# Two fused convolution layers on one core: another order for the first and the last image, the x1 chunks of both in places of their own, and one preparation step of every image a round earlier

## The reference, cut to what matters

```
# layer 0: x1 = x + conv0(group_norm(x)), with v = group_norm(x)
f     = relu(Wc @ v + bc)                         # 512 -> 128 channels (1x1)
gk1   = relu(mean(v) @ Wc.T + bc); g_kern = gk1 * Wkk + bkk
sk    = relu(Wc @ max_over_16x16_cells(v) + bc)   # 3x3 cells
dynW  = relu(Wck @ stack([g_kern, sk]) + bck)     # a 3x3 kernel of each image's own
y     = conv3x3(f, dynW) + b_ad                   # 128 -> 128
x1    = x + (Wf @ y + bf)                         # 128 -> 512 (1x1)
# layer 1: 32 groups of 16 channels, weights of each group's own
out   = x1 + conv3x3(group_norm(x1), kernels, groups=32)
```

## Time and profile before

| | us |
|---|---|
| median of three runs | 3616.0 (3615.7 to 3616.5) |
| the profiled execution | 3616.31 |
| its span, first to last instruction | 3614.6 |
| PE busy | 3498.8 (97%) |
| DVE busy | 2532.3 (70%) |
| ACT busy | 2109.9 (58%) |
| POOL busy | 965.3 (27%) |
| DMA, share of 16 engines | 68.5% |

### The profile page before, as it was taken

The page is one execution under the profiler, slowest core; times in us unless marked ns, Lnnn a source line. Parts: engine busy times, 40 slices in busy tenths (PEclk is TensorE's granted clock), DMA queues, the critical chain, the costliest instruction groups (busy, mean ns, idle before and its releaser), DMA issues.

```text
span 3614.6 us, 60228 instructions
## 1 busy us (share of the span) xinstructions
PE 3498.8 (97%) x18688; PEld 2789.1 (77%) x18688; DVE 2532.3 (70%) x5365; ACT 2109.9 (58%) x3559; POOL 965.3 (27%) x1039
## 2 busy tenths in 40 slices
PE   5799999999999999999999999999999999999996
PEld 4677877777877778877778777778777778777785
DVE  7676777776767677777667777767777777776742
ACT  4365555665555665655655556655556655556654
POOL 2033222232222232222332222322222322223323
PEclk9899999999999999999999999999999999999998
DMA  5467767677767667767677667677676777676666
GB/s 122 142 193 190 190 178 185 200 195 192 185 180 195 191 184 193 190 183 197 189 188 190 186 178 207 197 190 186 178 191 194 188 195 186 182 199 187 170 156 158
DMA packets 317577, 666.88 MB, mean 184 GB/s; under 512 B 58863, under 2 KB 288242, under 8 KB 288645
## 3 DMA queue, kind: packets, MB, share of 16 engines
q1 hardware_dynamic: 317317, 663.34, 68.5%
HBM read 355.00 MB, written 308.28 MB: 184 GB/s over the span
## 4 chain that ended last, share of the span: by engine, by line
PE 90%; issue 5%; DVE 4%; DMA 1%; POOL 0%; DVEq 0%; ACT 0%; SPq 0%; POOLq 0%; ACTq 0%
PE pb L853 15%; PE pb L855 15%; PE pb L854 15%; PE pac L853 7%; PE pd L853 7%; PE pd L855 7%; PE pd L854 7%; PE pac L854 6%; PE pac L855 6%; PE pac L925 2%; PE pac L862 1%; DVE x1b L764 1%; PE ps L918 1%; DMA big<-x 0%; DVE va L596 0%
## 5 line engine op out<-in xcount | busy, mean ns | idle before, releaser
L407 POOL TENSOR_TENSOR hl<-un,hl 128x384 f16<-128x384 f32 x1024 | 937.6, 916 | 2570.2 <-ACT hl L432 2566.6
L432 ACT ACTIVATE hl<-un 128x384 f16<-128x384 f32 x1024 | 539.0, 526 | 427.8 <-PE pb L855 361.7
L428 ACT ACTIVATE un<-big,b_t,s_t 128x384 f32<-128x384 f32 x1024 | 709.7, 693 | 16.1 <-DMA big<-x_rows 16.1
L853 PE MATMUL pb<-fh,dynh 128*128 128x480 f32 (+1 forms) x1440 | 548.2, 381 | 0.0
L855 PE MATMUL pb<-fh,dynl 128*128 128x480 f32 (+1 forms) x1440 | 545.3, 379 | 0.0
L854 PE MATMUL pb<-fl,dynh 128*128 128x480 f32 (+1 forms) x1440 | 544.4, 378 | 0.0
L774 DVE SCALAR_TENSOR_TENSOR big<-pd,kout,big 96x768 f32<-96x768 f32 x256 | 258.8, 1011 | 382.6 <-PE pd L855 382.6
L853 PE MATMUL pd<-hl,k_h 128*96 128x384 f16 x1536 | 507.0, 330 | 18.8 <-POOL hl L407 18.8
L774 DVE SCALAR_TENSOR_TENSOR big<-pb,kout,big 96x768 f32<-96x768 f32 x256 | 258.9, 1011 | 351.8 <-PE pb L855 351.8
L853 PE MATMUL pb<-hl,k_h 128*96 128x384 f16 x1536 | 504.9, 329 | 0.0
L854 PE MATMUL pd<-hl,k_h 128*96 128x384 f16 x1536 | 504.8, 329 | 0.0
(11 more groups left out here) (115 smaller groups left out, 5241.6 us busy)
## 6 DMA issues: line engine op xcount, KB each, us to landing
big<-x SPq DMA_DIRECT2D x128, 1152.0 KB, 9.8
x_rows<-x1b SPq DMA_DIRECT2D x128, 1152.0 KB, 5.6
big<-x_rows SPq DMA_DIRECT2D x128, 1152.0 KB, 12.7
out<-big SPq DMA_DIRECT2D x128, 1152.0 KB, 6.2
big<-x_rows SPq DMA_DIRECT2D x256, 192.0 KB, 13.2
x_rows<-mrow SPq DMA_DIRECT2D x64, 96.0 KB, 1.9
big<-kt SPq DMA_DIRECT2D x4, 288.0 KB, 9.7
big<-kt SPq DMA_DIRECT2D x2, 192.0 KB, 11.0
```

What stands on the lines that cost most here:

```text
L407: pool.tensor_tensor(hl[:, g % HL_RING, 1, :, 1:W + 1], un[:, g % U_RING], hl[:, g % HL_RING, 0, :, 1:W + 1], ALU.subtract).then_inc(hl_lo, 1)
L428: act.activation(un[:, g % U_RING], t_slot(g // GQ)[:, g % GQ], ACT.Identity, bias=b_t[:, g:g + 1], scale=s_t[:, g:g + 1]).then_inc(u_done, 1)
L432: act.activation(hl[:, g % HL_RING, 0, :, 1:W + 1], un[:, g % U_RING], ACT.Copy).then_inc(hl_hi, 1)
L853: pe.matmul(acc, high_w, high_x, start=start, stop=False)
```

## The change

It has three parts.

- **Step 0.** Its four chunks stand behind rounds 0 to 3 (`C_AT_FIRST`), ahead of the preparation of image 1. x1 of chunks 1 to 3 goes to the three tile buffers, so `residual` no longer waits for the DMA there; it waits for the split weights of layer 1 (`k_lo`), whose staging lies in those buffers, and still for `square`. The last maxima of image 0 and `centred` move behind the first `x_low`. `kernel_inputs` and the image's own kernel move on PE behind tiles 1 and 3 of stage A, with psum of their own (three banks of `pbd`, which joins `pb` and `pd`); `dyn_high`, `dyn_low` and the scale of layer 1's weights come behind stage A.
- **Step 31.** Its chunks stand behind rounds 0, 2, 4 and 6 (`C_AT_LAST`), with x1 in the free x places. Means, statistics, `write_means` and the tiles' loads of image 31 are issued in the rounds; two of its tiles go to x places. The last chunk is stored in four pieces.
- **Every step.** `centred` is a function of its own; a copy of 128x36 becomes one of 128x1. `prep_scaled` 0 and 1 go from round 10 to round 9, and `prep_scaled` 2 from round 11 to round 10.

The diff, cut:

```diff
@@ -48,6 +48,8 @@
...
 C_AT = {0: 0, 4: 1, 8: 2, 11: 3}
+C_AT_FIRST = {0: 0, 1: 1, 2: 2, 3: 3}
+C_AT_LAST = {0: 0, 2: 1, 4: 2, 6: 3}
...
+SQUARE_AFTER_LAST = {5: 0, 9: 1, 13: 2, 17: 3}
+SUMS_LAST = 7
+MEANS_LAST = 8
+GROUP_STATS_LAST = 10
+SPREAD_LAST = 12
...
-PREP_SCALED_AT = 10
+PREP_SCALED_AT = 9
...
@@ -225,7 +232,10 @@
...
-        dyn_acc = pac[:, :, 0:3 * CM]
+        def dyn_acc(n):
+
+            return pbd[:, 1:4, 0:3 * CM] if isinstance(n, int) and n == 0 else pac[:, :, 0:3 * CM]
...
+        def t_slot(n, c):
+
+            if is_step(n, N - 1):
+                if c < 2:
+                    at = 4 * PX + c * GQ * BW
+                    return x_flat[:, at:at + GQ * BW].rearrange("p (j b w) -> p j b w", j=GQ, w=W)
+                return tb[:, c - 1, :, :, :]
             return tb[:, T_SLOT[c], :, :, :]
+
+        def x1_home(n, c):
+
+            if is_step(n, 0) and c:
+                return tb[:, c - 1].rearrange("p j b w -> p (j b w)")[:, 0:OR_ * BW].rearrange("p (k m) -> p k m", k=OR_)
+            if is_step(n, N - 1) and c:
+                return xb[:, x_slot(c, 0), :].rearrange("p (k m) -> p k m", k=OR_)
+            return x1b[:, 0]
...
+        def chunks_of(d, more):
+            return C_AT_FIRST if not d else C_AT if more else C_AT_LAST
...
-                if T_SLOT[c] in T_SLOT[:c]:
+                if is_step(n, 0) and c < Q - 1:
+                    sp.wait_ge(x1_out[c + 1], 16)
+                    sp.wait_ge(sq_done, Q)
+                if is_step(n, N - 1):
+                    if c >= 2:
+                        sp.wait_ge(stored[c - 1], written)
+                elif T_SLOT[c] in T_SLOT[:c]:
                     sp.wait_ge(stored[T_SLOT.index(T_SLOT[c])], written)
                 else:
                     sp.wait_ge(stored[Q - 1 if c == 0 else c], written)
@@ -323,7 +361,13 @@
...
+            def store_pair(n, p):
+                at = 2 * p % GQ
+                sp.wait_ge(out_done, n * PAIRS + p + 1)
+                sp.dma_start(out[n, p // PER_CHUNK, :, at * BW:(at + 2) * BW],
+                             t_slot(n, p // PER_CHUNK)[0:M6, at:at + 2].rearrange("p j b w -> p (j b w)")).then_inc(stored[p // PER_CHUNK], 16)
...
-                if d:
+                    if d:
+                        store(n - 1, 0)
+                    write_x1(n, 1)
+                    if d:
+                        load_t(n - 1, Q - 1)
+                        store(n - 1, 1)
+                    write_x1(n, 2)
+                    if d:
+                        store(n - 1, 2)
+                    write_x1(n, 3)
+                else:
+                    write_x1(n, 1)
                     store(n - 1, 0)
-                write_x1(n, 1)
-                if d:
+                    write_x1(n, 2)
                     load_t(n - 1, Q - 1)
+                    write_x1(n, 3)
                     store(n - 1, 1)
-                write_x1(n, 2)
-                if d:
+                    write_means(n)
+                    load_t(n, 0)
+                    load_t(n, 1)
+                    load_t(n, 2)
                     store(n - 1, 2)
-                write_x1(n, 3)
+                    load_t(n, 3)
...
             store(N - 2, Q - 1)
-            write_means(N - 1)
             for c in range(Q - 1):
-                load_t(N - 1, c)
-            store(N - 1, 0)
-            load_t(N - 1, Q - 1)
-            for c in range(1, Q):
                 store(N - 1, c)
+            for p in range(PAIRS - PER_CHUNK, PAIRS):
+                store_pair(N - 1, p)
             for c in range(Q):
-                sp.wait_ge(stored[c], (N + 1 if c else N) * 16)
+                sp.wait_ge(stored[c], (N, N + 1, N + 1, N + PER_CHUNK)[c] * 16)
...
                         f_high(n, t - 1)
+                    if is_step(n, 0) and t == 2:
+                        act.wait_ge(const_in, CONSTS * 16)
+                        gate_rows(0)
                 f_high(n, NT - 1)
+                if is_step(n, 0):
+                    dyn_high(0)
...
-                    if g in SQUARE_AFTER:
-                        square(n, SQUARE_AFTER[g])
+                    squares = SQUARE_AFTER if more else SQUARE_AFTER_LAST
+                    if g in squares:
+                        square(n, squares[g])
...
-                square(n, Q - 1)
+                if more:
+                    square(n, Q - 1)
...
             root_first(0)
-            act.wait_ge(const_in, CONSTS * 16)
-            gate_rows(0)
             for i in range(AHEAD):
                 x_high(0, 0, i)
-            dyn_high(0)
...
             def prep_means(n):
-                vec.wait_ge(max_done, Q * (n + 1))
                 vec.wait_ge(bn_done, Q * (n + 1))
-                vec.tensor_copy(cent[:, :, 0:TAPS], mx[:, :, :])
+                vec.tensor_copy(va[:, 4, 0:1], bst[:, 0, 0, 0:1])
...
                 vec.tensor_tensor(va[:, 2, :], va[:, 1, :], mv[:, :, 1], ALU.add).then_inc(stat_ready, 1)
-                vec.tensor_tensor(cent[:, :, 0:TAPS], cent[:, :, 0:TAPS], negm[:, :].unsqueeze(2).to_broadcast([P, Q, TAPS]), ALU.add)
+
+            def centred(n):
+                vec.wait_ge(max_done, Q * (n + 1))
+                vec.tensor_tensor(cent[:, :, 0:TAPS], mx[:, :, :], negm[:, :].unsqueeze(2).to_broadcast([P, Q, TAPS]), ALU.add)
                 vec.tensor_copy(cent[:, :, TAPS:GATES], va[:, 0, :].unsqueeze(2).to_broadcast([P, Q, TAPS])).then_inc(cent_done, 1)
...
-                    else:
+                        if is_step(n, 1):
+                            for before in range(Q - 1):
+                                vec.wait_ge(x1_out[before], 16)
+                    elif is_step(n, 0):
+                        vec.wait_ge(k_lo, K_PARTS)
+                    elif not is_step(n, N - 1):
                         vec.wait_ge(x1_out[c - 1], (n + 1) * 16)
                     reached(vec, sq_done, n * Q + c)
...
+                if is_step(n, 0):
+                    dyn_low(0)
+                    kernel_maximum()
+                    kernel_scales()
...
+                    chunks = chunks_of(d, more)
+                    if r in chunks:
+                        for u in range(chunks[r] * OR_, (chunks[r] + 1) * OR_):
                             residual(n, odd, u)
+                    if not more:
+                        if r == SUMS_LAST:
+                            x1_means(n)
+                        if r == GROUP_STATS_LAST:
+                            x1_group_means(n)
+                            x1_variances(n)
...
-                    if r == X1_SUMS_AT:
+                            centred(n + 1)
+                    if more and r == X1_SUMS_AT:
                         x1_means(n)
...
-                maxima(0, 0, c)
+                if c < Q - 1:
+                    maxima(0, 0, c)
             prep_means(0)
-            kernel_maximum()
             prep_variances(0)
+            vec.wait_ge(const_in, CONSTS * 16)
             constants()
             for i in range(3):
                 prep_scaled(0, i)
             for i in range(AHEAD):
                 x_low(0, 0, i)
-            dyn_low(0)
+            maxima(0, 0, Q - 1)
+            centred(0)
             images(vec, step)
-            x1_group_means(N - 1)
-            x1_variances(N - 1)
...
                 pe.wait_ge(wc_done, n + 1)
-                pe.wait_ge(dyn_done, n + 1)
+                if not is_step(n, 0):
+                    pe.wait_ge(dyn_done, n + 1)
                 for t in range(NT):
                     a_tile(n, t)
+                    if is_step(n, 0) and t == 1:
+                        kernel_inputs(0)
+                    if is_step(n, 0) and t == 3:
+                        dyn_kernels(0)
+                if is_step(n, 0):
+                    pe.wait_ge(dyn_done, 1)
...
+                    chunks = chunks_of(d, more)
+                    if r in chunks:
+                        for u in range(chunks[r] * OR_, (chunks[r] + 1) * OR_):
                             c_unit(n, u)
-                    if r == PAIRS - 1:
+                    if r == (PAIRS - 1 if more else MEANS_LAST):
                         x1_group_means(n)
+                    if not more and r == SPREAD_LAST:
+                        x1_spread(n)
...
             group_variance(0)
             pe.wait_ge(vec_const, 2)
-            kernel_inputs(0)
-            dyn_kernels(0)
             images(pe, step)
-            x1_spread(N - 1)
```

More of the change, by code:

```diff
@@ L284, in load_x @@
             def load_x(n, odd, c):
-                if isinstance(n, int) and n == 1 and c in STATS_IN_B:
+                if is_step(n, 1) and c in STATS_IN_B:
                     sp.wait_ge(max_done, Q)
@@ L336, in step @@
                 if d:
-                    if isinstance(n, int) and n == 1:
+                    if is_step(n, 1):
                         sp.wait_ge(k_lo, K_PARTS)
@@ L484, in dyn_high @@
                 act.wait_ge(dyn_mm, n + 1)
```

(24 more changed lines are left out.)

27 lines of the change are left out of this document (16 added, 11 removed).

## The result

The changed kernel takes 3671.7 us (median of 4 runs, 3671.0 to 3672.6) against 3615.9 us of the kernel before (4 runs, 3613.8 to 3616.5): ratio 1.0154, 95% interval 1.0142 to 1.0166. It is slower, as forecast, but by 56 us and not by 17; the time lies above the range. The profiled execution has a span of 3669.3 us against 3614.6.

What follows compares the result with a forecast made beforehand. PE, busy 97% of the span with matmuls back to back, was taken to bound the kernel, so a change pays only where PE waits. Start, end and rounds summed to 3616.3 - 9 - 19.1 + 45 = 3633.2 us, range 3608 to 3656.

Steps and rivals of the forecast that it cites:

- The ends: Program start and end, each paid once: together 28.1 us gained, range 23 to 31.
- The last image: End of the program: PE restarts 16.6 us sooner and the smaller last store saves 2.5; 19.1 us gained, range 16 to 20.
- instead of 22: Gap ahead of the last sixteen pairs: expected to be 5 us in the changed kernel's profile instead of 22.
- The first: Start of the program, image 0 to stage A of image 1: 9 us gained, range 7 to 11.
- Stage B is unchanged: Image 0: stage B keeps its length, so the chunks start at 91.3 instead of 95.29.
- The delay a step: Steps 1 to 30, chunk 3's first residual: prep_scaled a round earlier delays it 1.5 us a step.
- PE has no slack there: all of it is added to the step: Rounds, output 11 and chunk 3's first residual: their later start, 1.0 us before POOL's holding, lengthens the step in full.
- 30 x 1.5 = 45 us lost: Rounds: the delay of 1.5 us a step, paid in 30 steps, costs 45 us, bounds 3 and 72.
- The bounds: Delay a step in the rounds: 0.1 if nothing were held by POOL, 2.4 if both wch and wcl were held to a subtraction's end.
- the highest of my cases, 3660: Rival for the rounds: wch and wcl both held to the end, 72 us lost, 3660 us; chance 0.12.
- The move works: Rival for the rounds: with a square root 1.8 us sooner, PE's wait shrinks 0.5 us a step, 3573 us; chance 0.08.
- the sign turning at 0.94 us a step: Rounds against ends: the change turns from gain to loss at a delay of 28.1 / 30 = 0.94 us a step.

Runs made afterwards that it cites:

- dyn_ahead: Changed kernel with, in image 0 alone, the dynamic kernels' halves (dyn_high, dyn_low) ahead of the last f tile's halves: 3667.6 us, ratio 1.0143.
- filled_wait: Changed kernel with 12 extra unused matmuls on PE in its wait ahead of chunk 3's fourth unit: 3636.9 us, ratio 1.0058.
- root_early: Changed kernel with the first statistics' square root ahead of group 23 on ScalarE and chunk 2's squares behind group 24, image 0 excepted: 3577.2 us, ratio 0.9894.
- dose1: Kernel before with one extra unused reduction on VectorE ahead of chunk 3's first residual in every image: 3634.0 us, ratio 1.0051.
- dose2: Kernel before with two extra unused reductions on VectorE ahead of chunk 3's first residual in every image: 3687.1 us, ratio 1.0197.
- before_scaled9: Kernel before with only PREP_SCALED_AT changed from 10 to 9, both ends as before: 3696.4 us, ratio 1.0223.
- best2: best1 plus unused PE matmuls (44, 14 and 12) in the waits between C of image 0 and A of image 1: 3567.2 us, ratio 0.9866.
- best1: Changed kernel with root_early's and dyn_ahead's edits and, in the last image, second square root and scale operations ahead of output 15: 3569.2 us, ratio 0.9872.

## Why the prediction was right or wrong

- *The ends.* Measured by themselves 24.8 us in the spans (27.6 in the medians) against 28.1. The last image was right: 18.9 against 19.1, with the restart, 4.9 us of wait ahead of it, as forecast (its "instead of 22" counts from the end of the rounds; the wait itself was 18.8). The first was mis-sized: 3.7 us at stage A of image 1 against 9 (range 7 to 11). Stage A at 37.58 (37.1) and stage B at 61.11 (60.3 to 60.6) were nearly right. What failed is "Stage B is unchanged": B ran 2.6 us longer (33.4 from its start to that of the chunks, it was 30.75 by the earlier trace rows), because the 3.0 us of idle PE that I had just put ahead of it brought the clock down; dyn_ahead showed it by taking the idle time away. The size is partly chance: with the same image 0, filled_wait has half of that low stretch and starts stage A of image 1 at 136.4, a gain of 5.8 and still below the range. Most of the rest is the preparation of image 1, of which I counted 8.1 us from `kernel_inputs` to stage A by the earlier trace rows; it took 138.48 - 128.20 = 10.3, with `kernel_inputs` 1.89 instead of 1.36 us and the kernel's products 4.17 instead of 2.77, at a clock of 0.59.
- *The delay a step.* 1.5 us forecast, 1.38 measured (110.88 less 109.5), and for the reason given: one of the two instructions was held by POOL (`wcl`, by 0.58 us) and the other was not, having started 0.02 us ahead of POOL's subtraction, and L713 waits 1.86 us for the square root. PE's wait came to 57.1 us where 60 were forecast.
- *The step that failed:* "PE has no slack there: all of it is added to the step", and after it "30 x 1.5 = 45 us lost". What is added is the delay and then what PE loses by having stood still. I used PE's granted clock at the start of the program, and expected the slow restart at the end, but priced the rounds at full clock, although the step that I wrote took PE's wait from 0.55 to 2.0 us. The runs showed that the wait is followed by 3.4 us at half the clock in 24 of 30 steps, 1.5 us each. The term is 30 x 1.38 + 24 x 1.5 = 77. With it the sum is 3616.3 - 28.1 + 77 = 3665.2, and with the start's missing 5.3 us 3670.5; the profiled execution took 3671.0.
- *The bounds.* 0.1 and 2.4 a step were bounds of DVE's delay. A bound on the time needed the clock's share on top of them, and the highest of my cases, 3660, was short for the same reason.
- *The rivals.* "The move works" described the right mechanism and the right condition, a square root 1.8 us sooner: with it root_early gave 3577 against the 3573 worked out. It needed only another place for one set of squares on ACT, which the change did not make. The reason that I gave for the sign turning at 0.94 us a step has to be restated too: the delay of dose1, 0.6 a step, brings no low clock, that of dose2, 1.2, brings it in 21 of 30 steps, so a delay of 0.94 may already cost more than itself. Where between the two the cost sets in was not measured.

## What to carry to other kernels

A delay handed to PE in a loop is not priced by its length alone: look whether PE's wait gets as long as one behind which this trace, or one like it, shows a lower granted clock, and add what the following stretch then loses (here 1.5 us for each 3.4 us at 0.5). When an instruction is moved ahead of one that an engine waits for, first see what the moved one itself waits for; here bringing its input forward turned a loss of 77 us in the rounds into a gain of 17 (3289.0 us in the kernel before, 3366.4 changed, 3271.9 in root_early). And two changes in one edit want to be timed apart: the ends were worth 25 to 28 us, and one number hid it.

## What the runs showed of the hardware

- A wait of PE of 1.8 to 2.0 us in otherwise dense matmuls was followed by 3.4 us at half the clock in 21 to 27 of 30 steps (21 in dose2, 22 in before_scaled9, 24 in the changed kernel, 27 in dyn_ahead); waits of 1.2 us never were (0 of 30 in dose1). In the same kernel, with the same wait in every step, some steps had it and some had not.
- A low stretch also began where PE had not waited: in best2, just behind six matmuls of 19 rows (2.20 us), with no wait over 0.3 us in the 18 us before. In best1 and dyn_ahead the same matmuls had none behind them.
- Twelve unused matmuls (1.59 us) in the wait removed all 24 low stretches, and the rounds took 33 us less. PE busy with nothing of use was faster than PE idle.
- VectorE and GpSimd held each other, and the one that started first was not held. `wcl` started while a subtraction ran and took 1.27 us, 0.69 with GpSimd idle. The cast `wch` started 0.02 us ahead of a subtraction and took 0.41, as alone, and the subtraction took 1.14 instead of 0.89. Both in all 30 steps.
